# MLP phase of a two-layer kernel: layer norm and transposes of a later image spread over the turn, product 1 three blocks ahead, response norm ahead of the last splits

## The chip, the cores and the metric

The kernel runs on one core of a Trainium2 chip. The metric is the device time of one execution in microseconds, lower is better; three runs of the kernel before took 5912.92, 5915.08 and 5927.24 us (median 5915.08). The engines are TensorE (PE), VectorE (DVE), ScalarE (ACT), GpSimd (POOL) and SyncE (SP), which issues most transfers.

## The reference

The first layer is a quantized window attention on 16 images of 192 channels and 56 x 56 pixels. The second layer, the one that is concerned here, is a ConvNeXt block. Of it the phase changed here computes everything behind the depthwise convolution:

```python
mu = mean(y, -1); var = mean(square(y - mu), -1)          # over 192 channels
y = (y - mu) * rsqrt(var + 1e-6) * ln_g + ln_b
y = einsum('bhwc,cf->bhwf', y, w1) + b1                   # 192 -> 768, product 1
y = gelu(y)
gx = sqrt(sum(square(y), (1, 2)))                         # per image and feature
nx = gx / (mean(gx, -1) + 1e-6)
y = grn_g * (y * nx) + grn_b + y                          # response norm
y = einsum('bhwf,fc->bhwc', y, w2) + b2                   # 768 -> 192, product 2
out = residual + y
```

## The kernel before, in words

Eight phases follow one another; the last, `phase_mlp`, starts at 4221 us of the profiled execution. In it an image is 3136 tokens, taken as seven chunks (n = 0 to 6) of 448 tokens, and the 768 features are six blocks (f = 0 to 5) of 128. To keep fp32 precision with 16-bit operands, values are split into a high and a low fp16 part, and a product is a sum over the parts.

The phase is a software pipeline over images. Turn i computes product 2 of image i, product 1 and GELU of image i+1, and the layer norm of image i+2. A prologue does images 0 and 1 up to that point; turn 0 is written out, turns 1 to 12 are a loop, turns 13 to 15 are written out again without the parts that have no image left (`turns`, with the flags `first`, `one`, `two`, `three`).

The five engines each run their own program in order, and meet by semaphores. In a turn:

- PE (`turn` under `blk.tensor`) does for each chunk a first half, t = 0, of 18 matmuls of product 2 for output rows 0 to 127 (L1521), and a second half, t = 1, in which each block has two matmuls of product 2 for the other rows and then five of product 1 of the next image (`product1`, L1486). A product 1 block y = 6n + f waits for GELU of block y-3, because `h_psum` has three buffers. At the start of the turn PE waits for all 42 low splits of image i and for the weights. `group` (L1470) transposes two columns of 128 tokens of the layer norm's result in 6 matmuls; 14 groups make an image. Groups 0 to 2 are issued in the first half of chunk 6, 3 to 5 in its second half, 6 to 13 behind it, with `mean` (L1491), a matmul that sums over features, between them.
- ACT does GELU (L1570) and the sum of squares (L1554) of each block, copies the low sum out of `out_psum` (`low_sum`, L1561) once a chunk, and places transposed groups (`place`, L1545). `gelu` of block y waits for the low split of block y-3, because there are three `gelu` buffers. `xT_psum` has two buffers, so group x waits until group x-2 is placed.
- DVE splits each GELU block into `gelu_hi` (L1685) and `gelu_lo` (L1688) in `split`, adds product 2 to the residual (`result`, L1724, two in a chunk, and `add_low_sum`, L1730), computes the layer norm's statistics (`stats`, L1613 and L1625) and applies them (`normalize`, L1635 and L1641, in seven steps, each a seventh of the image), and computes the response norm (`response_norm`, L1695 to L1707), which folds the factor into the weights of product 2 (`w_parts`).
- POOL computes the power -0.5 of the variances (L1428), the low parts of the layer norm's result (L1433), two operations for each normalize step, and the square root in the response norm (L1438), once in a turn.
- SP loads the image for the layer norm (`z_img`), loads the residual and stores the output.

`gelu_hi` and `gelu_lo` hold one image each. Block (n, f) of image i is read by product 2 in chunk n, and the split of image i+1 writes the same place. Before the change nothing waits for that read by itself: the product 1 whose GELU is split there stands behind the read on PE.

DVE's slots are numbered 0 to 13, two in a chunk: slot 2n stands ahead of the first `result` of chunk n, slot 2n+1 ahead of its splits. Statistics have slots 2 to 8, normalize steps slots 10, 10, 11, 11, 12, 12 and 13; the response norm follows the last `result`.

```python
for f in range(NF + 1):                       # split(m, n)
    y = NF * n + f
    if f < NF:
        dve.wait_ge(hd, NH * m + y + 1)
        v.tensor_scalar(hh[:, f, cols], h[y % 3][:], kh[:], None, ALU.mult).then_inc(hhd, 1)
    if f > 0:
        dve.wait_ge(hhd, NH * m + y)
        v.scalar_tensor_tensor(hl[:, f - 1, cols], h[(y - 1) % 3][:], kh[:], hh[:, f - 1, cols], ...)
```

## Time and profile before

| | |
|---|---|
| median of 3 runs | 5915.08 us (5912.92 to 5927.24) |
| the profiled execution, its time and its span | 5934.2 us, 5932.5 us |
| mean granted PE clock | 0.824 |
| `phase_mlp` in the span | 4221 to 5932 us |
| busy in 4500 to 5000 us: PE, DVE, ACT, POOL | 440.3, 437.0, 321.9, 103.3 us |
| PE waiting for placed groups (L1545), 4430 to 5400 us | 114.3 us in 30 waits |
| DVE waiting for GELU (L1570), same stretch | 70.3 us in 184 waits |

"Busy" counts the time in which at least one instruction of the engine is under way. A granted clock of 1.00 is 2.4 GHz, 0.50 is 1.2 GHz. In the timeline a row can stand for several instructions of one kind in a row (x2, x3); a duration includes the time in which an instruction drains while the next has begun, so the pace is read from one start to the next. What stands in brackets is the idle time ahead of a row and who ended it.

### The profile page before, as it was taken

The page shows a single profiled execution, that of the slowest core. Times are in us where ns is not written, and L with a number is a line of the kernel's source. Part 1 is how long each engine was busy: PE and PEld are TensorE (multiplying, and loading weights), DVE is VectorE, ACT ScalarE, POOL GpSimd, SP SyncE. Part 2 cuts the span into 40 slices and gives each one's busy share as a digit, 9 for nine tenths or more (in the row PEclk, how much of TensorE's full clock was granted, in tenths as well). Part 3 has the DMA queues.
Part 4 walks back from the last instruction along what each step waited for, and adds up shares of the span by engine and source line. Part 5 has one row for each costly group of instructions (what it writes and reads, how often), then busy time and mean ns, then how long its engine had stood idle before and what let it go on. Part 6 is the DMA issues. An engine that isn't in the chain of part 4 may idle for free. (4 is left out here: it accounts for less than half of the span.)

```text
span 5932.5 us, 106325 instructions
## 1 busy us (share of the span) xinstructions
PE 4236.2 (71%) x34250; PEld 2544.0 (43%) x34250; DVE 4572.3 (77%) x8672; ACT 3112.4 (52%) x5458; POOL 1554.1 (26%) x1645
## 2 busy tenths in 40 slices
PE   0888994555556666666664564999578989898988
PEld 0335552222235555455553443444344444444444
DVE  6998996999999889898896453000488888888885
ACT  0756660000057677676773564444366666666664
POOL 1104330000045555555554221000121211212120
PEclk9995555555589999999997777999789989898999
DMA  7755663333332232222323777788402121221212
GB/s 295 218 144 157 194 191 78 66 65 62 61 65 75 68 77 67 74 73 68 77 58 116 260 265 249 271 287 296 139 32 94 60 94 59 77 77 66 87 64 62
DMA packets 226352, 724.94 MB, mean 122 GB/s; under 512 B 34954, under 2 KB 132746, under 8 KB 205194
## 3 DMA queue, kind: packets, MB, share of 16 engines
q1 hardware_dynamic: 182346, 524.67, 30.7%
q0 software_dynamic: 43584, 195.21, 9.7%
q8 instruction: 197, 3.23, 0.2%
q14 instruction: 225, 1.84, 0.1%
HBM read 428.25 MB, written 291.50 MB: 121 GB/s over the span
## 5 line engine op out<-in xcount | busy, mean ns | idle before, releaser
L862 ACT ACTIVATE attn_int<-p_psum,scalars 128x588 int8<-128x588 f32 x512 | 384.7, 751 | 1175.3 <-PE p_psum L534 1174.2
L786 POOL TENSOR_TENSOR exp_lo<-exp,exp_hi 128x294 f16<-128x294 f32 x1024 | 827.3, 831 | 648.4 <-ACT exp_hi L856 646.8
L1570 ACT ACTIVATE gelu<-h_psum,b_rows,w_unscale 128x448 f32<-128x448 f32 x672 | 486.2, 724 | 509.1 <-PE h_psum L1486 345.6
L1521 PE MATMUL out_psum<-gelu_hi,w_parts 128*128 128x448 f16 x2016 | 621.5, 363 | 8.2 <-DVE w_parts L1707 4.4
L827 PE MATMUL o_psum<-a_v,exp_hi 128*128 128x68 f16 x3072 | 287.1, 202 | 447.2 <-DVE a_o L907 439.4
L534 PE MATMUL range_psum<-q_diag,k_diag 128*128 128x196 bf16 x1536 | 365.4, 374 | 330.3 <-DVE p_min L652 328.1
L1613 DVE BATCH_NORM_STATS2 ln_stats<-z_img 128x6 f32<-128x192 f32 x448 | 125.5, 337 | 548.0 <-DMA z_img<-zd 548.0
L1486 PE MATMUL h_psum<-ln_parts_T,w_hi 128*128 128x448 f16 x2016 | 501.1, 358 | 20.1 <-DVE w_in L1676 16.3
L881 DVE SCALAR_TENSOR_TENSOR logit_int<-attn_int,scalars,bias_products 128x588 f16<-128x588 int8 x512 | 445.9, 871 | 88.8 <-issue 56.9
L1283 PE MATMUL conv_psum<-c_in,toeplitz 128*128 128x448 f16 (+1 forms) x2304 | 469.2, 365 | 61.9 <-DMA dwb<-in_L_conv_dw_b_dram 61.9
L1521 PE MATMUL out_psum<-gelu_lo,w_parts 128*128 128x448 f16 x1344 | 484.7, 361 | 0.0
L1688 DVE SCALAR_TENSOR_TENSOR gelu_lo<-gelu,h_scale,gelu_hi 128x448 f16<-128x448 f32 x672 | 457.3, 694 | 0.0
L827 PEld LDWEIGHTS o_psum<-a_v,exp_hi 128*128 128x128 f16 x3072 | 221.8, 101 | 517.1 <-DVE a_o L907 480.2
L1685 DVE TENSOR_SCALAR gelu_hi<-gelu,h_scale 128x448 f16<-128x448 f32 x672 | 320.0, 485 | 141.1 <-ACT gelu L1570 130.3
L534 PEld LDWEIGHTS range_psum<-q_diag,k_diag 128*128 128x128 bf16 x1536 | 181.8, 160 | 513.5 <-DVE p_min L652 510.2
L855 ACT ACTIVATE exp<-l_psum,scalars 128x588 f32<-128x588 f32 x512 | 381.6, 745 | 22.5 <-PE l_psum L813 21.6
L856 ACT ACTIVATE exp_hi<-l_psum,scalars 128x588 f16<-128x588 f32 x512 | 392.7, 767 | 0.0
L652 DVE TENSOR_TENSOR p_max<-range_psum,p_max 128x588 f32<-128x588 f32 x512 | 387.2, 756 | 0.0
L652 DVE TENSOR_TENSOR p_min<-range_psum,p_min 128x588 f32<-128x588 f32 x512 | 387.1, 756 | 0.0
L1297 ACT ACTIVATE c_out<-conv_psum,dwb,conv_unscale 128x448 f32<-128x448 f32 x192 | 223.6, 1165 | 307.1 <-PE conv_psum L1283 307.1
L1554 ACT ACTIVATE gelu_square<-gelu 128x448 f32<-128x448 f32 x672 | 380.2, 566 | 0.0
L1486 PE MATMUL h_psum<-ln_parts_T,w_lo 128*128 128x448 f16 x1344 | 370.6, 358 | 0.0
(307 smaller groups left out, 9779.2 us busy)
## 6 DMA issues: line engine op xcount, KB each, us to landing
k_diag<-kd SPq DMA_DIRECT2D x128, 384.0 KB, 5.1
toeplitz<-gd SPq DMA_DIRECT2D x48, 1024.0 KB, 16.5
yd<-y_out POOLq DMA_DIRECT2D x16, 2880.0 KB, 26.9
c_in<-yd SPq DMA_DIRECT2D x24, 1920.0 KB, 9.2
zd<-c_out POOLq DMA_DIRECT2D x24, 1792.0 KB, 13.8
z_img<-zd SPq DMA_DIRECT2D x16, 2688.0 KB, 9.8
x_chunk<-in_x_dram SPq DMA_DIRECT2D x12, 3136.0 KB, 9.8
x_img<-in_x_dram SPq DMA_DIRECT2D x16, 2352.0 KB, 16.0
```

The source lines that it names most:

```text
L534: last = nc.tensor.matmul(out[:, g, 0:HG * N], kt[:, g].rearrange("p o n -> p (o n)")[:, j::UP], q[:, g, :, j * N:(j + 1) * N], start=True ...
L652: v.tensor_tensor(e[:], ps[:, j % 4, 0:G, 0:HG * N], e[:], op).then_inc(done, 1)
L786: last = nc.gpsimd.tensor_tensor(el[r][:, :, a, 0:N], src[:, :, a], eh[r][:, :, a, 0:N], ALU.subtract)
L827: last = nc.tensor.matmul(po[:, b * PV0:(b + 1) * PV0], x[r][:, b].rearrange("p a n -> p (a n)"), rhs, start=x is eh, stop=x is el)
L856: nc.scalar.activation(eh[r][:].rearrange("p b a n -> p a b n")[:, :, :, 0:N], pl[:, bank, 0:HM].rearrange("p (a b n) -> p a b n", a=2, b= ...
L862: nc.scalar.activation(a1[l % 2][:].rearrange("p (g n) -> p g n", g=G), pp[:, 0:G, 0:HG * N], ACT.Copy, scale=col(s, CP)).then_inc(a1d, 1)
L881: v.scalar_tensor_tensor(a2[r][:], a1[(l - LAG_A2) % 2][:], col(s, RAT), s.bpart[:], ALU.mult, ALU.add).then_inc(a2d, 1)
L1283: last = nc.tensor.matmul(out[:, :, lo:hi], tp[k][:, w, ch, 2 - d, :], yi[k][:, :, ch, yy, lo + d:hi + d], start=x == 0 and part == 0, sto ...
L1486: last = nc.tensor.matmul(ph[:, y % 3, 0:TCH], w, xx, start=x == 0, stop=x == 4)
L1521: last = nc.tensor.matmul(po[:, t, 0:TCH], w, hx[:, f, cols], start=f == 0 and x == 0, stop=f == NF - 1 and x == len(steps) - 1)
L1570: nc.scalar.activation(h[y % 3][:], ph[:, y % 3, 0:TCH], ACT.Gelu, scale=k1[:], bias=b1[:, f:f + 1]).then_inc(hd, 1)
L1688: v.scalar_tensor_tensor(hl[:, f - 1, cols], h[(y - 1) % 3][:], kh[:], hh[:, f - 1, cols], ALU.mult, ALU.subtract).then_inc(hld, 1)
```

## The change

Eight things change, all in `phase_mlp`.

- The layer norm of an image is spread. In the loop, normalize steps of image i+2 stand in slots 0 to 6, and statistics, now of image i+3, in slots 9, 9, 10, 10, 11, 11, 12. Turn 0 does the statistics of image 2 in slots 0 to 3, its normalize steps in slots 5 to 8, and the statistics of image 3 in slots 10 to 13.
- PE transposes groups 2k and 2k+1 behind product 1 blocks 6k+7 and 6k+9, at most one group behind a block, and ACT places them at the same block numbers. Group 13 stands behind the last block.
- Product 1 is issued three blocks earlier relative to product 2: behind block b of product 2 stands product 1 of block b+3, and behind the last three blocks stand blocks 0 to 2 of the image after. The prologue issues three blocks more.
- Each high split waits in addition until product 2 has read the same block of the image before (`block_read`, new semaphore `gelu_block_read`).
- Product 2 waits for the low splits of its own chunk, not of the whole image.
- ACT copies the low sum of chunk n behind GELU of block 6n+8, three blocks later.
- The response norm stands behind split 3 of chunk 6; splits 4 and 5 follow the last `result`. PE's `mean` stands behind block 4 of chunk 6.
- SP issues the next `z_img` load behind the store of chunk 2 (3 in turn 0), not at the end of the turn.

```diff
-        EARLY0, EARLY, MEAN_AT = 3, 6, 10
-        TURN_STATS, TURN_NORM = 2, (10, 10, 11, 11, 12, 12, 13)
+        AHEAD, LAST = 3, 4
+        STATS_AT, NORM_AT, NEXT_STATS_AT = (0, 0, 1, 1, 2, 2, 3), (5, 5, 6, 6, 7, 7, 8), (10, 10, 11, 11, 12, 12, 13)
+        TURN_NORM_AT, TURN_STATS_AT = range(LG), (9, 9, 10, 10, 11, 11, 12)
+        group_at = [NF * (x // 2 + 1) + 1 + 2 * (x % 2) for x in range(NG)]
+        first_group_at = [max(at, 4 * NF - 2 + x) for x, at in enumerate(group_at)]
...
+                    if three and n == (3 if first else 2):
+                        sp.wait_ge(xnd, ROWP * i + 3 * ROWP)
+                        zload(i + 3)
...
-                if three:
-                    sp.wait_ge(xnd, ROWP * i + 3 * ROWP)
-                    zload(i + 3)
...
             def turn(i, first, one, two, three):
+                if first:
+                    deviation(i + 2)
                 if two:
-                    normalize(i + 2)
+                    low_parts(i + 2)
+                if three:
+                    deviation(i + 3)
                 if one:
                     root(i + 1)
...
-                if y == 0:
-                    pe.wait_ge(xtd, NG * m + NG)
+                if f == 0:
+                    pe.wait_ge(xtd, NG * m + 2 * n + 2)
...
+            for y in range(AHEAD):
+                product1(1, y, False)
+
+            def ahead(i, y, first, one, two):
+
+                if y < NH:
+                    if one:
+                        product1(i + 1, y, False)
+                elif two:
+                    product1(i + 2, y - NH, False)
+                for x in range(NG):
+                    if two and y == min((first_group_at if first else group_at)[x], NH + AHEAD - 1):
+                        group(i + 2, x, False)
 
             def turn(i, first, one, two, three):
-                pe.wait_ge(hld, NH * i + NH)
                 pe.wait_ge(w2d, 2 * i + 1)
                 for n in range(NTC):
                     cols = slice(n * TCH, (n + 1) * TCH)
+                    pe.wait_ge(hld, NH * i + NF * n + NF)
                     for t in range(2):
                         y = 2 * n + t
...
-                            if one and t == 1:
-                                product1(i + 1, NF * n + f, False)
-
-                            if two and y == MT - 2 and f >= NF - EARLY0:
-                                group(i + 2, f - (NF - EARLY0), False)
-                            if two and y == MT - 1 and f < EARLY - EARLY0:
-                                group(i + 2, EARLY0 + f, False)
-                for x in range(EARLY, NG + 1):
-                    if one and x == MEAN_AT:
-                        mean(i + 1)
-                    if two and x < NG:
-                        group(i + 2, x, False)
+                            elif t == 1:
+                                last.then_inc(ofd, 1)
+                            if t == 1:
+                                ahead(i, NF * n + f + AHEAD, first, one, two)
+                            if one and y == MT - 1 and f == NF - 2:
+                                mean(i + 1)
...
             def turn(i, first, one, two, three):
-                for y in range(NH):
-                    n, f = y // NF, y % NF
-                    if two and y == NH - NF:
-                        for x in range(EARLY0):
+                at = first_group_at if first else group_at
+                for y in range(NH + AHEAD):
+                    if one and y < NH:
+                        gelu(i + 1, y, False)
+                    if y == NH + AHEAD - 1:
+                        low_sum(i, NTC - 1, first)
+                    for x in range(NG):
+                        if two and y == min(at[x], NH + AHEAD - 1):
                             place(i + 2, x)
-                    if one:
-                        gelu(i + 1, y, False)
-                    if f == NF - 1:
+                    n = (y - NF + 1 - AHEAD) // NF
+                    if y % NF == (NF - 1 + AHEAD) % NF and 0 <= n < NTC - 1:
                         low_sum(i, n, first)
-                    if two and n == NTC - 1 and f < EARLY - EARLY0:
-                        place(i + 2, EARLY0 + f)
-                if two:
-                    for x in range(EARLY, NG):
-                        place(i + 2, x)
...
+                if not (isinstance(m, int) and m == 0):
+                    dve.wait_ge(trd, NG * m - NG + 2 * x + 2)
...
-                if x == 0 and not early:
-                    dve.wait_ge(trd, NG * m)
...
-            def split(m, n):
+            def block_read(i, n, f):
+
+                if f < NF - 1:
+                    dve.wait_ge(ofd, (NF - 1) * (NTC * i + n) + f + 1)
+                else:
+                    dve.wait_ge(om, MT * i + 2 * n + 2)
+
+            def split(m, n, before=None, lo=0, hi=NF):
 
                 cols = slice(n * TCH, (n + 1) * TCH)
-                for f in range(NF + 1):
+                for f in range(lo, hi + 1):
                     y = NF * n + f
-                    if f < NF:
+                    if f < hi:
                         dve.wait_ge(hd, NH * m + y + 1)
+                        if before is not None:
+                            block_read(before, n, f)
                         v.tensor_scalar(hh[:, f, cols], h[y % 3][:], kh[:], None, ALU.mult).then_inc(hhd, 1)
-                    if f > 0:
+                    if f > lo:
...
-            def response_norm(m):
+            def response_norm(m, before=None):
...
+                    if before is not None:
+                        block_read(before, NTC - 1, fs.stop - 1)
                     glink(v.tensor_copy(w2p[:, fs, 0:C], w2f[:, fs]))
...
-            def layernorm(m, slot):
-                if TURN_STATS <= slot < TURN_STATS + LG:
-                    stats(m, slot - TURN_STATS)
+            def layernorm(i, slot, first, two, three):
                 for x in range(LG):
-                    if TURN_NORM[x] == slot:
-                        normalize(m, x, False)
+                    if first and STATS_AT[x] == slot:
+                        stats(i + 2, x)
+                    if two and (NORM_AT if first else TURN_NORM_AT)[x] == slot:
+                        normalize(i + 2, x, False)
+                    if three and (NEXT_STATS_AT if first else TURN_STATS_AT)[x] == slot:
+                        stats(i + 3, x)
 
             def turn(i, first, one, two, three):
                 for n in range(NTC):
-                    if two:
-                        layernorm(i + 2, 2 * n)
+                    layernorm(i, 2 * n, first, two, three)
                     if n > 0:
                         add_low_sum(i, n - 1)
                     result(i, 2 * n)
-                    if two:
-                        layernorm(i + 2, 2 * n + 1)
+                    layernorm(i, 2 * n + 1, first, two, three)
                     if one:
-                        split(i + 1, n)
+                        split(i + 1, n, i, 0, NF if n < NTC - 1 else LAST)
+                    if one and n == NTC - 1:
+                        response_norm(i + 1, i)
                     result(i, 2 * n + 1)
                 if one:
-                    response_norm(i + 1)
+                    split(i + 1, NTC - 1, i, LAST)
                 add_low_sum(i, NTC - 1)
```

Three places show the new order, in the loop's turn; names in brackets are what the instruction waits for.

PE at the end of the turn, before: the last product 1 block of chunk 6 (`h_psum`), then the groups (`xT_psum`) and the mean matmul.

```order
L1486 MATMUL h_psum<-ln_parts_T,w_hi 128x448 [waits gelu_done]
L1486 MATMUL h_psum<-ln_parts_T,w_hi 128x448 x2
L1486 MATMUL h_psum<-ln_parts_T,w_lo 128x448 x2
L1465 REGISTER_ALU
L1467 REGISTER_ALU [waits ln_lo_done]
L1470 MATMUL xT_psum<-ident_f,ln_parts 128x128 [waits xT_placed]
L1470 MATMUL xT_psum<-ident_f,ln_parts 128x128 x5
L1467 REGISTER_ALU
L1470 MATMUL xT_psum<-ident_f,ln_parts 128x128 [waits xT_placed]
...
L1490 ISA
L1491 MATMUL mean_psum<-grn_sum,ones_f 128x1 [waits grn_chain]
```

The same place in the changed kernel, from the next to last group to the end of the loop.

```order
L1483 MATMUL xT_psum<-ident_f,ln_parts 128x128 [waits xT_placed]
L1483 MATMUL xT_psum<-ident_f,ln_parts 128x128 x5
L1503 ISA
L1504 MATMUL mean_psum<-grn_sum,ones_f 128x1 [waits grn_chain]
L1547 MATMUL out_psum<-gelu_hi,w_parts 128x448
L1547 MATMUL out_psum<-gelu_lo,w_parts 128x448
L1499 MATMUL h_psum<-ln_parts_T,w_hi 128x448 [waits gelu_done]
L1499 MATMUL h_psum<-ln_parts_T,w_hi 128x448 x2
L1499 MATMUL h_psum<-ln_parts_T,w_lo 128x448 x2
L1480 REGISTER_ALU
L1483 MATMUL xT_psum<-ident_f,ln_parts 128x128 [waits xT_placed]
L1483 MATMUL xT_psum<-ident_f,ln_parts 128x128 x5
```

The mean matmul stands ahead of the last two product 2 matmuls, and one group is left behind them.

ACT at the seam of chunks 0 and 1, before; the numbers are those of the three `gelu` buffers, `w1_rows<-out_psum` is the low sum.

```order
L1570 ACTIVATE gelu0<-h_psum,b1_rows,w1_unscale 128x448 [waits squares_done,gelu_lo_done,h_product]
L1554 ACTIVATE gelu_square0,sum_squares<-gelu2 128x448 [waits squares_done,gelu_done]
L1565 REGISTER_ALU
L1570 ACTIVATE gelu1<-h_psum,b1_rows,w1_unscale 128x448 [waits squares_done,gelu_lo_done,h_product]
L1554 ACTIVATE gelu_square1,sum_squares<-gelu0 128x448 [waits squares_done,gelu_done]
L1565 REGISTER_ALU
L1570 ACTIVATE gelu2<-h_psum,b1_rows,w1_unscale 128x448 [waits squares_done,gelu_lo_done,h_product]
L1554 ACTIVATE gelu_square0,sum_squares<-gelu1 128x448 [waits squares_done,gelu_done]
L1558 ISA
L1560 REGISTER_ALU [waits out_product]
L1561 COPY w1_rows<-out_psum 64x448 [waits out_whole]
```

The changed kernel: `gelu0` to `gelu2` here are blocks 6 to 8 of the next image, so the low sum of chunk 0 stands behind the third GELU of chunk 1, with a placed group ahead.

```order
L1590 ACTIVATE gelu0<-h_psum,b1_rows,w1_unscale 128x448 [waits squares_done,gelu_lo_done,h_product]
L1574 ACTIVATE gelu_square1,sum_squares<-gelu2 128x448 [waits squares_done,gelu_done]
L1590 ACTIVATE gelu1<-h_psum,b1_rows,w1_unscale 128x448 [waits squares_done,gelu_lo_done,h_product]
L1574 ACTIVATE gelu_square0,sum_squares<-gelu0 128x448 [waits squares_done,gelu_done]
L1562 ISA
L1565 COPY ln_parts_T<-xT_psum 128x3x224 [waits x_transposed]
L1590 ACTIVATE gelu2<-h_psum,b1_rows,w1_unscale 128x448 [waits squares_done,gelu_lo_done,h_product]
L1574 ACTIVATE gelu_square1,sum_squares<-gelu1 128x448 [waits squares_done,gelu_done]
L1578 ISA
L1580 REGISTER_ALU [waits out_product]
L1581 COPY w1_rows<-out_psum 64x448 [waits out_whole]
```

The low sum moved behind three more GELU blocks, and a group is placed between.

DVE at the end of the turn, before: the last splits, the last `result`, then the response norm (`grn_factor` to `w_parts`) and the low sum.

```order
L1684 REGISTER_ALU
L1685 TENSOR_SCALAR gelu_hi<-gelu,h_scale 128x448 [waits gelu_done]
L1688 SCALAR_TENSOR_TENSOR gelu_lo<-gelu,h_scale,gelu_hi 128x448 [waits gelu_hi_done] x2
L1721 REGISTER_ALU
L1724 SCALAR_TENSOR_TENSOR residual<-out_psum,out_unscale,residual 64x448 [waits out_product]
L1695 TENSOR_REDUCE grn_factor<-sum_squares 128x6 [waits squares_done]
...
L1707 TENSOR_TENSOR w_parts<-w_scaled,w_parts 128x3x128
L1727 REGISTER_ALU
L1730 SCALAR_TENSOR_TENSOR residual<-w_rows,out_unscale,residual 64x448 [waits out_done,low_sum_copied]
```

The changed kernel: the response norm begins behind low split 3, and two high and two low splits follow it.

```order
L1712 TENSOR_SCALAR gelu_hi<-gelu,h_scale 128x448 [waits gelu_block_read]
L1715 SCALAR_TENSOR_TENSOR gelu_lo<-gelu,h_scale,gelu_hi 128x448 [waits gelu_hi_done] x2
L1721 REGISTER_ALU
L1722 TENSOR_REDUCE grn_factor<-sum_squares 128x6 [waits squares_done]
...
L1736 TENSOR_TENSOR w_parts<-w_scaled,w_parts 128x3x128
L1753 SCALAR_TENSOR_TENSOR residual<-out_psum,out_unscale,residual 64x448 [waits out_product]
L1699 REGISTER_ALU [waits gelu_done]
L1712 TENSOR_SCALAR gelu_hi<-gelu,h_scale 128x448 [waits gelu_block_read]
L1712 TENSOR_SCALAR gelu_hi<-gelu,h_scale 128x448 [waits out_product,gelu_done]
L1715 SCALAR_TENSOR_TENSOR gelu_lo<-gelu,h_scale,gelu_hi 128x448 [waits gelu_hi_done] x2
L1759 SCALAR_TENSOR_TENSOR residual<-w_rows,out_unscale,residual 64x448 [waits out_done,low_sum_copied]
```

Splits 4 and 5 and the last `result` moved behind the response norm, and each high split has two waits.

## Rows read from the trace of the kernel before

**Rows 1.** POOL timeline, once-a-turn operation. Columns: start us, duration us, engine, line, operation.
```profile
4459.35 1.33 POOL L1438 TENSOR_TENSOR grn_x<-grn_factor,exponents 128x6 f32<-128x6 f32 x1 [6.08 <-DVE grn_factor L1695]
...
5790.56 1.32 POOL L1438 TENSOR_TENSOR grn_x<-grn_factor,exponents 128x6 f32<-128x6 f32 x1 [6.08 <-DVE grn_factor L1695]
5880.08 1.32 POOL L1438 TENSOR_TENSOR grn_x<-grn_factor,exponents 128x6 f32<-128x6 f32 x1 [88.19 <-DVE grn_factor L1695]
```

**Rows 2.** PE timeline, chunk 5 and the start of chunk 6 of turn 6.
```profile
5034.89 0.54 PE L1521 MATMUL out_psum<-gelu_hi,w_parts 128*128 128x448 f16 x2
...
5038.67 0.73 PE L1486 MATMUL h_psum<-ln_parts_T,w_hi 128*128 128x448 f16 x3
...
5046.24 0.54 PE L1521 MATMUL out_psum<-gelu_hi,w_parts 128*128 128x448 f16 x2
```

**Rows 3.** DVE timeline, end of the prologue, then turn 6.
```profile
4358.75 0.56 DVE L1641 CAST ln_parts<-ln_out 128x768 f16<-128x768 f32 x1
...
5006.44 1.12 DVE L1613 BATCH_NORM_STATS2 ln_stats<-z_img 128x6 f32<-128x192 f32 x4
...
5007.76 0.78 DVE L1685 TENSOR_SCALAR gelu_hi<-gelu,h_scale 128x448 f16<-128x448 f32 x2
...
5035.85 0.45 DVE L1685 TENSOR_SCALAR gelu_hi<-gelu,h_scale 128x448 f16<-128x448 f32 x1 [0.28 <-ACT gelu L1570]
5036.22 1.27 DVE L1688 SCALAR_TENSOR_TENSOR gelu_lo<-gelu,h_scale,gelu_hi 128x448 f16<-128x448 f32 x2
5037.41 0.67 DVE L1724 SCALAR_TENSOR_TENSOR residual<-out_psum,out_unscale,residual 64x448 f32<-64x448 f32 x1
...
5049.27 1.71 DVE L1685 TENSOR_SCALAR gelu_hi<-gelu,h_scale 128x448 f16<-128x448 f32 x2
5050.90 1.08 DVE L1688 SCALAR_TENSOR_TENSOR gelu_lo<-gelu,h_scale,gelu_hi 128x448 f16<-128x448 f32 x1
...
5057.33 1.24 DVE L1635 TENSOR_SCALAR ln_out<-z_img,ln_mean_var,ln_rstd 128x192 f32<-128x192 f32 x4
...
5059.07 2.43 DVE L1635 TENSOR_SCALAR ln_out<-z_img,ln_mean_var,ln_rstd 128x192 f32<-128x192 f32 x4
...
5073.62 0.18 DVE L1695 TENSOR_REDUCE grn_factor<-sum_squares 128x6 f32<-128x42 f32 x1
...
5079.19 0.75 DVE L1704 TENSOR_TENSOR w_scaled<-w_in,grn_factor 128x576 f32<-128x576 f32 x1
```

**Rows 4.** PE timeline, the end of turn 6 and the next turn's start.
```profile
5048.51 0.50 PE L1470 MATMUL xT_psum<-ident_f,ln_parts 128*128 128x128 f16 x6
...
5057.05 0.82 PE L1470 MATMUL xT_psum<-ident_f,ln_parts 128*128 128x128 f16 x6 [6.57 <-ACT ln_parts_T L1545]
...
5079.40 0.92 PE L1521 MATMUL out_psum<-gelu_hi,w_parts 128*128 128x448 f16 x2 [0.37 <-DVE w_parts L1707]
```

**Rows 5.** Windows view: window us, length, PE busy (instructions), granted clock, DMA share, GB/s.
```profile
5057.00:5061.00 4.00, 3.95 (x20) 0.50 0.00 0
```

**Rows 6.** POOL timeline, one normalize step's two low parts.
```profile
5049.43 2.07 POOL L1433 TENSOR_TENSOR ln_parts<-ln_out,ln_parts 128x512 f16<-128x512 f32 x2 [1.08 <-DVE ln_parts L1641]
```

**Rows 7.** ACT timeline, turn 6, chunks 5 and 6.
```profile
5035.71 0.56 ACT L1554 ACTIVATE gelu_square<-gelu 128x448 f32<-128x448 f32 x1
...
5036.40 0.53 ACT L1561 COPY w_rows<-out_psum 64x448 f32<-64x448 f32 x1
...
5052.07 0.72 ACT L1570 ACTIVATE gelu<-h_psum,b_rows,w_unscale 128x448 f32<-128x448 f32 x1 [8.32 <-issue]
...
5053.25 0.71 ACT L1570 ACTIVATE gelu<-h_psum,b_rows,w_unscale 128x448 f32<-128x448 f32 x1
...
5062.61 0.72 ACT L1570 ACTIVATE gelu<-h_psum,b_rows,w_unscale 128x448 f32<-128x448 f32 x1 [0.20 <-PE h_psum L1486]
...
5064.39 0.73 ACT L1570 ACTIVATE gelu<-h_psum,b_rows,w_unscale 128x448 f32<-128x448 f32 x1
```

**Rows 8.** Page, DMA issues: transfer, queue, count, KB each, us from issue to landing.
```profile
z_img<-zd SPq DMA_DIRECT2D x16, 2688.0 KB, 9.8
```

12 lines of the change are left out of this document (8 added, 4 removed).

## The prediction

> **What bounds the kernel now.** I read the views in this order: the POOL timeline for the length of a turn, the PE timeline for its inner rhythm, then what ended PE's idle time, and last the DVE and ACT timelines beside it. The seven earlier phases end at 4221 us and are not touched, so only the last phase counts. Its turns are told apart by the POOL operation that occurs once in each [rows 1]: thirteen periods take 1331.2 us, 102.4 us each, and the one after them, without layer norm, 89.5 us.
>
> Inside a turn PE works through seven chunks. A chunk is 11.35 us from start to start [rows 2]: 3.4 us of product 2 for output rows 0 to 127 (first half), then six blocks of 1.325 us, in each two matmuls of product 2 (0.38 us) and five of product 1 (0.95 us) (second half). DVE, by contrast, may be far behind: the splits of chunk 5 begin at 5049.27 [rows 3], three microseconds after PE has left that chunk, and PE lost nothing in the chunk by it. PE runs at its rate in five chunks of seven; the time above the rate is at the end of the turn, where it waits 6.57 us for a transpose group [rows 4], again while ACT places groups, and then for the response norm. The clock then stands at 0.50, the 1.2 GHz level, for 4 us of product work [rows 5]. Seven chunks at the rate are 79.5 us and fourteen transpose groups 4.6 us (0.33 each: 0.50 busy, less the 0.17 by which a matmul's record outlasts its issue) [rows 4]: 84.1 of 102.4 us.
>
> **What the change removes.** The lump at the end goes: no PE wait on placed groups, and the squares and the response norm no longer wait for splits 40 and 41. Before, the stretch from the start of chunk 6 to the next turn is 5046.24 to 5079.40, 33.2 us [rows 2, 4]; chunk 0 behind it, partly at 1.2 GHz, takes 12.5 us (102.4 less 33.2 less five chunks).
>
> **What it adds.** PE issues product 1 of block b+3 behind block b. The rings stay at three `h_psum` and three `gelu` buffers, so that product waits for gelu b, and gelu b waits for low split b-3. At block 3 of a chunk (b counted within it) PE therefore waits for the low split of block 0 of the same chunk. Before, product b waited for gelu b-3 and so for low split b-6: a whole chunk of slack, which the lateness of 5049.27 used. PE is in order, so blocks 4 and 5 of product 2 stand behind the waiting product, and DVE's high splits 4 and 5 now wait for these two to be read. Each engine waits for the other once in a chunk. ACT, too, places a group after gelu 1 of a chunk and copies the low sum only after gelu 2, and the second half's product 2 waits for that copy.
>
> **The walk through a steady turn.** Time 0 is the end of PE's issue of the chunk before. Durations, start to start: high split 0.37, low split 0.59, result 0.59 [rows 3]; one stats step 1.32 [rows 3]; one normalize step 1.74 alone (5057.33 to 5059.07), 2.95 straight behind another (2.43 + 0.5) and, with two residual operations between, the middle of these, 2.35 [rows 3], since POOL's low parts of the step before run some 2 us beside it [rows 6]; gelu to gelu on ACT 1.78 with a placed group between, 1.17 without [rows 7].
> - DVE is free at 1.44: product 2 of block 5 is complete at -0.75, then high, low, low, result (2.15).
> - The low sum is copied at 4.13: low split 4 ends 0.34, gelu 1 at 0.43, square and group to 2.22, gelu 2, square, copy of 0.53. PE's second half starts there, not at 3.41: 0.7 us in chunks 1 to 6.
> - From the first high split (S) to PE's product at block 3: two highs and a low, gelu 0.72 and the hops between: 2.28 us, or 3.59 with POOL busy (5049.27 to the gelu of 5052.07 is 2.80, plus 0.79) [rows 3, 7]. Behind it PE needs 3.94 us, and 0.45 more where a placed group delays gelu 4.
>
> Chunk 0: DVE comes 5.3 late from the response norm (second weight half 2.3 [rows 3], result, four splits, low sum); normalize 7.0, result 7.6, normalize S = 10.0; 10.0 + 3.59 + 3.94 = 17.5.
> Chunks 1 and 2: normalize 3.2; low sum from 4.13 to 5.1 (a residual operation with two SBUF inputs beside POOL, taken like the low split, 1.08 for 0.68 [rows 3]); result 5.7; normalize S = 7.45; + 3.59 + 4.39 = 15.4 each.
> Chunk 3: one normalize, S = 5.7, no wait: 4.13 + 7.95 + two groups 0.66 = 12.7.
> Chunk 4: result 5.3, two stats steps (the first without aggregates) S = 7.65; + 2.28 + 4.39 = 14.3.
> Chunk 5: four stats steps, S = 7.95; 14.6.
> Chunk 6: second half from 4.13, product 2 of block 3 read at 9.0, low split 2 done 10.1, gelu 41 and both squares from there, 1.17 + 0.66 [rows 7], to 12.0; from the sum of squares to PE's next turn 5.78 us (5073.62 to 5079.40 [rows 3, 4]): 17.8.
> Sum: 17.5 + 30.8 + 12.7 + 14.3 + 14.6 + 17.8 = 107.8 us (107.9 unrounded).
>
> **The clock.** In chunk 0 PE stands still for 3.6 to 5 us before block 3. After 6.57 us of idling it ran at 1.2 GHz for 4 us, costing 1.9 [rows 4, 5]. Bounds 0 and 1.9 per turn; that wait is shorter than the row's, so I take the middle, 1.0. A steady turn is then 108.9, 6.5 above before; twelve of them +78.
>
> **The other turns.** Turn 0 does the layer norm of two images. Its statistics now stand ahead of everything, and their `z_img` load is issued when DVE's last normalize before it ends, near 4358.7 [rows 3]; at 9.8 us to landing [rows 8] DVE is held to about 4368.8. The same walk gives chunks of 16.1, 13.1, 16.1, 21.8, 15.0, 14.8 and 18.4, and 1 for the clock: end at about 4480.6, against 4465.0 before (5079.40 less six periods): +16. Turn 13 has no statistics: 105.4 against 102.3, +3. Turn 14 has no layer norm and no groups, its chunks run at 11.35 and only chunk 6 pays (16.8): 85.5 against 89.5, -4. Turn 15 is the same. The prologue's three early products (2.9 us) lie in the wait for `z_img`.
>
> Nothing for the load of image i+3: it is issued 4.8 us into chunk 3, lands 9.8 later, and its first statistics are 18 us into that chunk. The second wait of each high split I take at zero when it is met: ACT's gelu has three waits and keeps a pitch of 1.17 [rows 7]; the upper end is the hop of 0.09 from low split to gelu for each of 42, 3.8 us a turn, and is in the range.
>
> Total +78 + 16 + 3 - 4 = +93. The profiled execution took 5934.2 us (span 5932.5 and 1.7 around it) and would take 6027; it lay 19.1 above the median, and I put the change on the median: 5915.1 + 93 = 6008 us.
>
> **A rule to weigh.** A low split beside POOL took 1.08 us in place of 0.68 [rows 3], and I charged the low sum of chunks 1 and 2 the same 0.4. The Trainium skill ("SBUF — State Buffer", section "SBUF: two separate sides") says that the pair of ports that VectorE and GpSimd share is locked for a whole instruction, by VectorE also for two SBUF inputs. By that rule the low sum could be held until POOL is through, up to 0.3 us longer in each of the two chunks, and the sum would be about 7 us higher; the trace's 1.08 shows a partial hold and not which of the two it would be here.
>
> **Rivals.**
> 1. *Each engine is limited by its own work.* If the ring of three gives enough slack, a turn costs DVE's own work (splits 40.3, results and low sums 12.4, stats 9.6, normalizes with their delays 19.5, response norm 7.9, total 89.7) and some 4 us at the seam: 94. For it: before, DVE's lateness cost PE nothing in the middle chunks. Against it: that slack was six blocks and is now three. 12 x -8.4, turn 0 +6, turns 13 and 14 -14: -109, 5806 us. Faster; chance 0.14.
> 2. *The waits partly close.* If the spread steps meet POOL's low parts less than the rows suggest (2.28 for 3.59 and no 0.4), chunks 0, 1 and 2 lose 1.3, 1.7, 1.7; if the low sum also comes 0.7 earlier in chunks 1 to 6, the turn is about 101 to 103. With turn 0 that is 5905 to 5940, centre 5922. For it: the POOL rows overlap only where steps are close. Against: the walk puts them as close as before. Chance 0.16.
> 3. *The clock falls in every waiting chunk.* Chunks 1, 2, 4 and 5 wait 1 to 3.4 us each; if each then ran 4 us at 1.2 GHz, 6 to 8 us a turn come on top: 6008 + 84 = 6092. It decides from the point where 2 to 3 us of waiting is enough; the rows show the fall only after 6.57. Chance 0.08.
> 4. *My walk, with terms off by some tenths per chunk:* 108.9 +- 3 a turn, 5965 to 6050. Chance 0.62.
>
> **Numbers.** Predicted 6008; the range 5905 to 6060 takes in the last and most of the second, leaving out the first, and much of the third. A measurement of this kernel cannot tell less than 0.3% (18 us) from none. Slower: 0.62 + 0.08 + 0.07 of the second = 0.77; same 0.06; faster 0.14 + 0.03 = 0.17.
>
> **What the profile after would show.** Right: the POOL period near 109; PE's largest waits at the product-1 line, ended by ACT's gelu, once a chunk in chunks 0, 1, 2, 4, 5; DVE's high split waiting for product 2; the PE wait for placed groups gone. Wrong: a period below 102, PE waiting chiefly for the weight parts and DVE busy without gaps; or a second half that starts at 3.4 us, which would refute the low-sum term; or high splits beside POOL of 0.45 us, which would refute the port term.

## The result and the profile after

The changed kernel took 6057.5 us, median of 3 runs (6049.7 to 6058.9), against 5915.1: ratio 1.0231, 95% interval 1.0206 to 1.0257. It is slower, as forecast. The forecast was 6008 us in a range of 5905 to 6060; the measured 142 us are half as much again as the 93 predicted, and the time lies only 2.5 us inside the upper end of the range. The 5915.1 is a median of three runs; in the later comparisons the same kernel had medians of 5929 to 5933 us (7 to 21 runs each), so up to some 16 of the 142 us may lie in those three runs.

The profiled execution took 6058.85 us, 124.7 more than that of before. First the length of a turn, from the POOL timeline, to be laid beside [rows 1] (columns: start us, duration us, engine, line, operation):

```profile
4323.90 1.38 POOL L1445 TENSOR_TENSOR grn_x<-grn_factor,exponents 128x6 f32<-128x6 f32 x1 [63.95 <-DVE grn_factor L1722]
4469.46 1.32 POOL L1445 TENSOR_TENSOR grn_x<-grn_factor,exponents 128x6 f32<-128x6 f32 x1 [1.49 <-DVE grn_factor L1722]
...
5810.86 1.32 POOL L1445 TENSOR_TENSOR grn_x<-grn_factor,exponents 128x6 f32<-128x6 f32 x1 [4.36 <-DVE grn_factor L1722]
5917.77 1.32 POOL L1445 TENSOR_TENSOR grn_x<-grn_factor,exponents 128x6 f32<-128x6 f32 x1 [45.82 <-DVE grn_factor L1722]
6004.58 1.32 POOL L1445 TENSOR_TENSOR grn_x<-grn_factor,exponents 128x6 f32<-128x6 f32 x1 [85.49 <-DVE grn_factor L1722]
```

Turn 0 is 145.6 us long (before 127.2), the twelve steady turns 1341.4 or 111.8 each (before 102.4), then 106.9 (102.3) and 86.8 (89.5). The differences, +18.4, +112.5, +4.6 and -2.7, make +133 us in this phase. The first of these POOL operations came 8 us earlier in this execution than before: the layer norm of the phase's start came 9 us earlier, behind stages that are the same in both, and what follows it took 1 us more.

What ended the waits, from 4800 to 5600 us, seven turns (columns: engine, operation, what it waited for; us in total, times, longest; rows of PE and DVE, others left out at the dots):

```profile
PE h_psum L1499 <- ACT gelu L1590: 90.3, 63, 6.9
DVE gelu_hi L1712 <- PE out_psum L1547: 65.6, 99, 2.2
DVE residual L1759 <- ACT w_rows L1581: 42.0, 35, 2.9
...
PE out_psum L1547 <- ACT w_rows L1581: 22.9, 42, 0.8
...
PE mean_psum L1504 <- DVE grn_sum L1724: 21.3, 8, 2.7
...
DVE ln_out L1655 <- issue: 12.9, 8, 1.7
```

The wait for placed groups [rows 4] is gone. In its place PE waits at product 1 for ACT's gelu, and DVE's high split waits for PE: each for the other, as foretold. The PE timeline shows where (turn 6; the idle time before a row stands in brackets):

```profile
5028.58 0.59 PE L1504 MATMUL mean_psum<-grn_sum,ones_f 128*128 128x1 f32 x2 [2.67 <-DVE grn_sum L1724]
...
5032.56 0.55 PE L1547 MATMUL out_psum<-gelu_hi,w_parts 128*128 128x448 f16 x2 [0.37 <-DVE w_parts L1736]
...
5047.95 1.30 PE L1499 MATMUL h_psum<-ln_parts_T,w_hi 128*128 128x448 f16 x3 [6.93 <-ACT gelu L1590]
...
5054.00 0.54 PE L1547 MATMUL out_psum<-gelu_hi,w_parts 128*128 128x448 f16 x2
...
5058.07 0.36 PE L1547 MATMUL out_psum<-gelu_hi,w_parts 128*128 128x448 f16 x1 [0.50 <-ACT w_rows L1581]
...
5064.78 0.74 PE L1499 MATMUL h_psum<-ln_parts_T,w_hi 128*128 128x448 f16 x3 [1.85 <-ACT gelu L1590]
...
5069.19 0.54 PE L1547 MATMUL out_psum<-gelu_hi,w_parts 128*128 128x448 f16 x2
...
5084.38 0.54 PE L1547 MATMUL out_psum<-gelu_hi,w_parts 128*128 128x448 f16 x2
...
5097.08 0.54 PE L1547 MATMUL out_psum<-gelu_hi,w_parts 128*128 128x448 f16 x2
...
5111.74 0.54 PE L1547 MATMUL out_psum<-gelu_hi,w_parts 128*128 128x448 f16 x2
...
5126.25 0.54 PE L1547 MATMUL out_psum<-gelu_hi,w_parts 128*128 128x448 f16 x2
...
5144.23 0.62 PE L1547 MATMUL out_psum<-gelu_hi,w_parts 128*128 128x448 f16 x2 [0.40 <-DVE w_parts L1736]
```

Chunk 0 starts at 5032.56; the rows at 5054.00, 5069.19, 5084.38, 5097.08, 5111.74 and 5126.25 are the first product 2 matmuls of chunks 1 to 6, and the last row is the start of the next turn. The second half of chunk 1 starts at 5058.07, 4.07 behind its first.

| chunk | 0 | 1 | 2 | 3 | 4 | 5 | 6 |
|---|---|---|---|---|---|---|---|
| predicted, us | 17.5 (+1.0 clock) | 15.4 | 15.4 | 12.7 | 14.3 | 14.6 | 17.8 |
| measured, us | 21.4 | 15.2 | 15.2 | 12.7 | 14.7 | 14.5 | 18.0 |

Six chunks of seven lie within 0.4 us of the walk. Chunk 0 is 2.9 longer than its 18.5. The DVE timeline, to be laid beside [rows 3], shows one part of that:

```profile
5037.16 0.67 DVE L1759 SCALAR_TENSOR_TENSOR residual<-w_rows,out_unscale,residual 64x448 f32<-64x448 f32 x1
5039.46 1.25 DVE L1655 TENSOR_SCALAR ln_out<-z_img,ln_mean_var,ln_rstd 128x192 f32<-128x192 f32 x4 [1.62 <-issue]
...
5041.81 2.06 DVE L1655 TENSOR_SCALAR ln_out<-z_img,ln_mean_var,ln_rstd 128x192 f32<-128x192 f32 x4
...
5044.38 1.71 DVE L1712 TENSOR_SCALAR gelu_hi<-gelu,h_scale 128x448 f16<-128x448 f32 x2
5046.00 1.08 DVE L1715 SCALAR_TENSOR_TENSOR gelu_lo<-gelu,h_scale,gelu_hi 128x448 f16<-128x448 f32 x1
...
5050.79 0.45 DVE L1712 TENSOR_SCALAR gelu_hi<-gelu,h_scale 128x448 f16<-128x448 f32 x1 [1.71 <-PE out_psum L1547]
...
5058.05 0.89 DVE L1759 SCALAR_TENSOR_TENSOR residual<-w_rows,out_unscale,residual 64x448 f32<-64x448 f32 x1 [0.82 <-ACT w_rows L1581]
```

Before its first normalize DVE idles 1.62 us for nothing but "issue". The first high split therefore starts 11.8 us into the turn, and not at 10.0. Turn 1, the loop's first, is the control: it has no such gap (PE row of its start, then DVE rows):

```profile
4474.89 0.93 PE L1547 MATMUL out_psum<-gelu_hi,w_parts 128*128 128x448 f16 x2 [0.73 <-DVE w_parts L1736]
```

```profile
4480.00 1.24 DVE L1655 TENSOR_SCALAR ln_out<-z_img,ln_mean_var,ln_rstd 128x192 f32<-128x192 f32 x4
...
4484.91 1.71 DVE L1712 TENSOR_SCALAR gelu_hi<-gelu,h_scale 128x448 f16<-128x448 f32 x2
```

Its first high split starts 10.0 us in, as predicted. In turn 6, behind PE's stall the high split waits 1.71 for PE in turn. The windows view shows the other part (granted clock: third number from the right):

```profile
5029.00:5030.00 1.00, 1.00 (x4) 0.43 (x5) 0.62 (x4) 0.00 (x0) 0.00 (x0) 0.50 0.00 0
...
5032.00:5033.00 1.00, 0.63 (x7) 0.28 (x5) 1.00 (x2) 0.72 (x1) 0.00 (x0) 1.00 0.00 0
...
5048.00:5049.00 1.00, 1.00 (x3) 0.38 (x4) 1.00 (x3) 1.00 (x4) 0.00 (x0) 0.50 0.00 0
...
5052.00:5053.00 1.00, 1.00 (x10) 0.68 (x9) 0.00 (x0) 1.00 (x2) 0.00 (x0) 0.87 0.00 0
```

Behind the wait of 6.93 us PE works at 1.2 GHz until about 5052: product 1 and two blocks take 6.05 us (5047.95 to 5054.00) where 3.94 were reckoned. Together 1.8 + 2.1 - 1.0 (the clock term of the sum) = 2.9 us. Over the twelve steady turns chunk 0 takes 19.2 us in turn 1 and 20.7 to 22.3 in the others, 21.5 in the mean, 3.0 above 18.5.

### The profile page after: what moved, and what is told of

It is laid out like the page before. It is cut to its first block and busy times, and to the rows that moved or that the text cites. A ratio compares the mean times of both kernels' runs of the same rounds, so it can differ in the third digit from the quotient of the medians.

```text
span 6056.8 us, 107252 instructions
## 1 busy us (share of the span) xinstructions
PE 4259.9 (70%) x34250; PEld 2508.2 (41%) x34250; DVE 4540.7 (75%) x8672; ACT 3073.2 (51%) x5458; POOL 1556.1 (26%) x1645
## 3 DMA queue, kind: packets, MB, share of 16 engines
q14 instruction: 226, 1.85, 0.1%
## 5 line engine op out<-in xcount | busy, mean ns | idle before, releaser
L1499 PE MATMUL h_psum<-ln_parts_T,w_hi 128*128 128x448 f16 x2016 | 514.2, 365 | 205.3 <-ACT gelu L1590 186.8
L1440 POOL TENSOR_TENSOR ln_parts<-ln_out,ln_parts 128x512 f16<-128x512 f32 x224 | 231.2, 1052 | 661.5 <-DVE ln_parts L1659 661.5
L855 ACT ACTIVATE exp<-l_psum,scalars 128x588 f32<-128x588 f32 x512 | 381.7, 745 | 23.6 <-PE l_psum L813 22.3
```

The lines of the kernel that those rows point to most:

```text
L1499: last = nc.tensor.matmul(ph[:, y % 3, 0:TCH], w, xx, start=x == 0, stop=x == 4)
```

## The experiments

Ratios are to the kernel before, run on the same chip; "a turn" is the mean of the twelve steady ones in the profiled execution, from the once-a-turn POOL operation as above. The lead is the number of blocks by which product 1 is issued ahead of product 2; the response norm is early when it stands ahead of splits 4 and 5 of chunk 6, and last when it stands behind them.

| kernel | lead | gelu buffers | response norm | a turn, us | ratio (95%) |
|---|---|---|---|---|---|
| before | 0 | 3 | last | 102.4 | 1 |
| changed | 3 | 3 | early | 111.8 | 1.0231 (1.0206 to 1.0257) |
| ahead2 | 2 | 3 | early | 102.8 | 1.0012 (0.9999 to 1.0025) |
| ahead1 | 1 | 3 | early | 100.7 | 0.9958 (0.9937 to 0.9978) |
| ahead0 | 0 | 3 | early | 102.6 | 1.0014 (0.9997 to 1.0031) |
| spread_only | 0 | 3 | last | 102.1 | 1.0005 (0.9987 to 1.0023) |
| gelu_ring6 | 3 | 6 | early | 94.2 | 0.9837 (0.9815 to 0.9859) |
| lead1_gelu6 | 1 | 6 | early | 97.5 | 0.9901 (0.9870 to 0.9933) |
| gelu6_norm_last | 3 | 6 | last | 95.9 | 0.9879 (0.9855 to 0.9904) |
| gelu6_low_early | 3 | 6 | early | 94.5 | 0.9823 (0.9798 to 0.9848) |
| before_gelu6 | 0 | 6 | last | 102.3 | 0.9996 (0.9979 to 1.0013) |
| low_early | 3 | 3 | early | 109.2 | 1.0161 (1.0137 to 1.0186) |
| pool_light | 3 | 3 | early | 107.0 | 1.0129 (1.0110 to 1.0148) |
| norm_later | 3 | 3 | early | 110.9 | 1.0199 (1.0169 to 1.0229) |

**The lead.** Three kernels change one number (with lead 0 the mean's product also moves behind the last block, since it needs every gelu).

```diff
-        AHEAD, LAST = 3, 4
+        AHEAD, LAST = 2, 4        # ahead2; 1 in ahead1, 0 in ahead0
```

> Lead of two blocks (AHEAD 2). Ring theory: the wait moves from block 3 to block 4 of a chunk, 1.325 us less behind it in five chunks, and up to 1 us for the clock: 104 to 106 us a turn, total 5950 to 5975 us. Spread theory: no change of more than 10 us from 6057.

> Lead of one block (AHEAD 1). Ring theory: product 1 behind block b waits for low split b-5, so only block 5 of a chunk can wait for a split of the same chunk; what is left behind the wait is 2.65 us shorter than with a lead of three in each of chunks 0, 1, 2, 4, 5: 13 us a turn off, and 1 to 2 for the clock: 97 to 100 us, total 5860 to 5900 us. Spread theory: no change of more than 10 us from 6057.

> Product 1 again directly behind its own block (AHEAD 0), the mean behind the last of them; spread layer norm and early response norm kept. Ring theory (the three-block lead in rings of three costs the time): the wait inside each chunk goes, a turn is DVE's own work plus the seam, 93 to 97 us for 112.2, total 5810 to 5870 us. Rival, spread theory (the spread normalize steps beside POOL's low parts and the shifted response norm cost the time, not the lead): a turn stays at 107 us or more, total 6000 or more.

The spread theory falls with all three: with the normalize steps and the response norm where the change put them, a turn is 9 to 11 us shorter as soon as the lead is. The first step, from three to two, gave 9.0 us (102.8 a turn, 104 to 106 expected); the next gave only 2.1 more (100.7, with 97 to 100 expected), and the last took 1.9 back. All three totals missed what was expected: 5940, 5908 and 5941 us for 5950 to 5975, 5860 to 5900 and 5810 to 5870. A lead of one with three buffers is 0.4% faster than the kernel before. Here the ring theory, as I had it, failed: it expected 93 to 97 us for lead 0. The rows of ahead0 show what was overlooked (PE, then DVE timeline):

```profile
4919.23 0.36 PE L1547 MATMUL out_psum<-gelu_hi,w_parts 128*128 128x448 f16 x1 [1.87 <-DVE residual L1753]
```

```profile
4879.31 0.20 DVE L1722 TENSOR_REDUCE grn_factor<-sum_squares 128x6 f32<-128x42 f32 x1 [2.36 <-ACT gelu_square L1574]
...
4915.69 0.45 DVE L1712 TENSOR_SCALAR gelu_hi<-gelu,h_scale 128x448 f16<-128x448 f32 x1 [0.75 <-ACT gelu L1590]
```

PE stands nowhere at product 1, and it waits for DVE's residual operation instead (61.8 us in 32 waits from 4800 to 5600 us): DVE is the bound. But DVE itself waits, up to 0.75 for a gelu (47.1 us in 77 waits, some 6 us a turn) and 2.36 for the last square. With three buffers gelu b needs low split b-3 whatever the lead is. I read the waits so, that ACT can't get ahead of DVE when a group has to be placed, and that the work of the two engines adds up at these places; a run with no lead and six buffers, which would test it, is missing.

spread_only takes the early response norm away too, so that of the change the spread layer norm, the spread groups and the waits that go with them are left. Expected were 101 to 102 us a turn and a ratio of 0.995 to 1.001; measured were 102.1 and 1.0005. Spreading by itself neither costs nor gains here.

**The ring.** Six gelu buffers, with nothing else of the order changed. With nothing moved they do not fit: 192 bytes a partition are lacking (4608 needed for the last buffer, 4416 left). The room comes from one buffer of squares, laid into `w1_rows`, and half a `w2_scaled`; the number must divide the 42 blocks of an image.

```diff
-        h = [sb(f"gelu{k}", [P, TCH], F32) for k in range(3)]
+        h = [sb(f"gelu{k}", [P, TCH], F32) for k in range(6)]
...
-                if not (early and y < 3):
-                    act.wait_ge(hld, NH * m + y - 2)
+                if not (early and y < 6):
+                    act.wait_ge(hld, NH * m + y - 5)
```

> Lead of three kept, six gelu buffers for three (the room comes from one buffer of squares, placed in the unused w1_rows, and a w_scaled half as long; the h_psum ring stays at three). Ring theory: gelu b then waits for low split b-6, as many blocks back as with no lead and three buffers, so PE no longer stands inside the chunks and high splits 4 and 5 no longer wait for product 2. What is left of a turn is DVE's row of work: 88.5 us busy in every trace so far, 1.6 of loop turn-around, 1.5 + 0.35 + up to 2.4 in the response norm: 93 to 97 us for 112.2, total 5830 to 5880 us. Rival, PSUM theory (the three h_psum banks, with product 1 queued in front of product 2, are the limit whatever stands behind them): the PE wait at product 1 stays and the total is within 30 us of 6057.

Measured: 94.2 us a turn, ratio 0.9837, where the lead of three with three buffers had 1.0231. The PSUM theory falls: the three `h_psum` banks are the same, and PE's wait at product 1 is gone from the list. DVE is now back to back (timeline, chunk 0 of a turn):

```profile
4944.82 1.71 DVE L1712 TENSOR_SCALAR gelu_hi<-gelu,h_scale 128x448 f16<-128x448 f32 x2
4946.45 1.09 DVE L1715 SCALAR_TENSOR_TENSOR gelu_lo<-gelu,h_scale,gelu_hi 128x448 f16<-128x448 f32 x1
4947.46 0.44 DVE L1712 TENSOR_SCALAR gelu_hi<-gelu,h_scale 128x448 f16<-128x448 f32 x1
4947.82 0.67 DVE L1715 SCALAR_TENSOR_TENSOR gelu_lo<-gelu,h_scale,gelu_hi 128x448 f16<-128x448 f32 x1
4948.42 0.44 DVE L1712 TENSOR_SCALAR gelu_hi<-gelu,h_scale 128x448 f16<-128x448 f32 x1
```

A block costs it 0.96 us from high split to high split, without a bracket; and the windows view gives 87.4 us of DVE work in a stretch of 94.2 (fourth number; PE's, the second, is 87.2):

```profile
4928.00:5022.20 94.20, 87.19 (x499) 46.27 (x500) 87.43 (x212) 64.25 (x147) 20.53 (x16) 0.96 0.24 78
```

Ten idle gaps of DVE, from 0.24 to 1.78 us, make up the other 6.8 us; the two longest are the one before the first normalize and the 1.50 for POOL in the response norm.

Is it the buffers alone? And what do lead and norm add once the ring is six long?

> The kernel before with six gelu buffers (room made in the same way), nothing else changed. Ring theory of the pair (the lead makes the ring matter; the lump of layer norm, groups and response norm at the end is what holds the kernel before): product 1 behind block b waits there for low split b-6 already, so PE's waits for the groups and the weight parts stay: 100 to 102.4 us a turn, ratio to before 0.98 to 1.00. Rival (the gain of six buffers belongs to the buffers alone and the change adds nothing to it): a turn of 96 us or less, ratio 0.987 or lower with the end lump hidden.

> Lead of one block with six gelu buffers (low split b-8 is waited for). With three buffers this lead had 100.7 us a turn, of which DVE waited some 5 for gelus and 2.4 for the last square. Ring theory: with three more buffers ACT runs ahead of DVE and both go: 93 to 96 us a turn, total 5810 to 5860 us. If DVE's gelu waits come from the order of PE and ACT and not from the ring (rival), the turn stays at 100 to 101 and the total at 5900 to 5915.

> Lead of three and six gelu buffers, but the response norm again behind the last splits, and the mean's product behind the last block (LAST 6). In the lead-three ring-of-six kernel DVE is the bound, 94.1 us a turn, and PE waits 1.0 for the mean, 1.7 and 0.5 for the weight parts and 3.7 for a residual operation of DVE a chunk later. If DVE stays the bound, the later weights only shorten that later wait: 94 to 96 us a turn, ratio to before 0.983 to 0.988. Rival (the early response norm is what lets the lead pay): DVE itself waits for PE's first half of the next turn, 98 us a turn or more, ratio 0.992 or more.

The kernel before gains nothing from six buffers (0.9996). PE's waits for placed groups do fall there, from 91.4 to 23.4 us in 4800 to 5600 us, but once a turn PE waits for DVE in their place (PE timeline, chunk 6):

```profile
5059.28 0.55 PE L1521 MATMUL out_psum<-gelu_hi,w_parts 128*128 128x448 f16 x1 [6.34 <-DVE residual L1726]
```

DVE, with the normalize steps in a lump, has no gap from 5040 to 5075 us, and the weight parts come no sooner. So this lump holds the turn, whatever the number of buffers. The whole change loses 2.3% without the buffers; together they give 1.6%. With the ring of six a lead of three beats a lead of one by 0.6% (my expectation of 93 to 96 for lead one missed; PE there waits up to 4.0 for the mean, and DVE 2.6 for the last square, which a lead of three hides). The early response norm is worth 0.4%, between my two bounds: DVE stays the bound, but its gap before the first normalize grows from 1.9 to 2.8 at most, and its small waits for PE become more. How much of the 1.0% of lead one belongs to the lead and how much to the spread was not tried, as no run has six buffers and no lead.

**The parts of the walk.** The low sum, moved one gelu ahead; POOL's low parts cut to a quarter; the normalize steps half a chunk later.

```diff
# low_early
-                    n = (y - NF + 1 - AHEAD) // NF
-                    if y % NF == (NF - 1 + AHEAD) % NF and 0 <= n < NTC - 1:
+                    n = (y - NF + 2 - AHEAD) // NF          # and ahead of the placed groups
+                    if y % NF == (NF - 2 + AHEAD) % NF and 0 <= n < NTC - 1:
# pool_light: this leaves out part of the computation
-                    src, rows = xn[x % 2], slice(4 * x, 4 * x + 4)
+                    src, rows = xn[x % 2][:, 0:n], slice(4 * x, 4 * x + n)      # n = 1 from image 2
# norm_later
-        TURN_NORM_AT = range(LG)
+        TURN_NORM_AT = range(1, LG + 1)
```

> As the changed kernel (lead 3, three buffers), but ACT copies a chunk's low sum one gelu earlier, ahead of the placed group. By the walk of the prediction the second half of product 2 starts 0.5 to 0.7 us earlier in chunks 1 to 6, and the low sum's residual operation with it, which sets the first high split: 3 to 4 us a turn, total 6000 to 6025 us. If the low sum is not on the path (DVE held by its own work or by PE's stall alone), less than 10 us.

> As the changed kernel, but from image 2 on POOL computes the low parts of only one row in four of each layer norm step (the others keep older values: this leaves out part of the computation). Port theory (VectorE operations beside POOL's low parts are stretched, and the ring passes the whole delay on): the second normalize of a pair falls from 2.07 to about 1.25, two high splits from 1.71 to 0.80, a low split from 1.08 to 0.68, so chunks 0, 1, 2 each lose about 2.1 to 2.4 us and chunk 3 about 1: 7 to 8 us a turn, total 5950 to 5970 us. If POOL's company costs little, under 20 us.

> As the changed kernel (lead 3, three buffers), each normalize step half a chunk later: chunk 0 has one of them and chunk 3 two. Walk: DVE's first high split of chunk 0 comes 2.5 us earlier, PE's 6.9 us wait there shrinks to about 4.4; chunk 3 turns from 13.0 to about 15.2. If the wait of 6.9 us is what drops the clock in chunk 0, and 4.4 does not, another 2 us go: 110 us a turn, total 6030, ratio to before 1.018 to 1.020. If the clock stays as it is: 112 us, total 6050 to 6060, ratio 1.022 to 1.025.

low_early: 2.6 us a turn less, 0.7% by the ratios (some 41 us); slightly under 3 to 4, and its 6031 us miss the 6000 to 6025, but far over the rival's 10 us in total: the late low sum is on the path. Its PE rows have no wait for `w_rows` left, and part of the gain comes back at block 3 (2.02 there in place of 1.85). The rest of what is missing is the clock: chunk 1 of a turn takes 14.7 us and chunk 2, with the same wait, 15.9 (both 15.2 in the changed kernel), as it runs at 1.2 GHz behind it (PE and windows rows, chunk 2):

```profile
5074.62 0.98 PE L1499 MATMUL h_psum<-ln_parts_T,w_hi 128*128 128x448 f16 x3 [2.02 <-ACT gelu L1590]
```

```profile
5076.00:5078.00 2.00, 2.00 (x6) 0.76 (x5) 0.87 (x2) 2.00 (x6) 0.00 (x0) 0.50 0.00 0
```

This happens in one waiting chunk of each of the twelve turns (chunk 1 in two of them, chunk 2 in ten) and costs 1.2 to 1.4 us. Without it the gain would have been 3.8 us a turn, within the expectation.

pool_light: 4.8 a turn less, for 7 to 8 expected. Its chunk 1 (PE timeline, to be laid beside the wait of 1.85 above):

```profile
5040.33 0.36 PE L1547 MATMUL out_psum<-gelu_hi,w_parts 128*128 128x448 f16 x1 [0.50 <-ACT w_rows L1581]
5045.73 0.74 PE L1499 MATMUL h_psum<-ln_parts_T,w_hi 128*128 128x448 f16 x3 [0.55 <-ACT gelu L1590]
...
5054.21 0.36 PE L1547 MATMUL out_psum<-gelu_hi,w_parts 128*128 128x448 f16 x1 [0.50 <-ACT w_rows L1581]
```

The chunk is 13.9 us long for 15.2. High split pair (0.98 for 1.71), low split (0.72 for 1.08) and low sum (0.68 for 0.89) give 1.3 us, which is that difference. My expectation had charged the second normalize of chunks 1 and 2 too; its rows are 1.23 there with and without POOL's load, since operations lie between it and the first. Only in chunk 0 does it meet POOL (2.06). Chunk 3 does not change (12.7), as PE is its bound.

norm_later: 110.9 us a turn, between the two expectations, and its interval overlaps that of the changed kernel, so the total tells nothing. The turns do, for behind the first of the twelve (108.2) they fall into two kinds, 109.4 to 109.6 and 110.8 to 112.4. PE and windows rows of one of 110.8 and one of 109.6:

```profile
5191.66 1.30 PE L1499 MATMUL h_psum<-ln_parts_T,w_hi 128*128 128x448 f16 x3 [4.24 <-ACT gelu L1590]
...
5401.52 0.93 PE L1547 MATMUL out_psum<-gelu_hi,w_parts 128*128 128x448 f16 x2 [1.40 <-DVE w_parts L1736]
...
5414.45 0.74 PE L1499 MATMUL h_psum<-ln_parts_T,w_hi 128*128 128x448 f16 x3 [2.73 <-ACT gelu L1590]
```

```profile
5192.00:5194.00 2.00, 2.00 (x7) 0.88 (x6) 1.05 (x2) 2.00 (x7) 0.00 (x0) 0.50 0.27 58
...
5402.00:5404.00 2.00, 2.00 (x7) 0.78 (x6) 1.88 (x4) 0.73 (x1) 0.00 (x0) 0.50 0.01 4
...
5414.00:5416.00 2.00, 1.55 (x9) 0.82 (x10) 1.61 (x4) 2.00 (x6) 0.00 (x0) 1.00 0.41 82
```

In the second, PE begins the turn at 1.2 GHz, so it reaches block 3 later, waits 2.73 and finds the full clock behind the wait. In the first it began at 2.4 GHz, waited 4.24 and worked at 1.2 GHz behind that. Here a slow clock ahead of the wait was absorbed by the wait, and one behind it was paid in full.

**The best version.**

> Lead of three, six gelu buffers, and the low sum copied one gelu earlier. DVE is the bound at 94.1 us a turn; its waits for the low sum and behind it for product 2 (0.71 and 0.73 in chunk 3) and for the reading of product 2 (0.2 to 0.6 each, some ten a turn) are what this can take: 92.5 to 93.5 us a turn, ratio to before 0.980 to 0.983. If they only move to another place of the chunk: 94.1, ratio 0.984.

Measured 0.9823, a turn 94.5. The two intervals (0.9798 to 0.9848 and 0.9815 to 0.9859) can't be told apart, and the turns are no shorter: with DVE as the bound its small waits move to another place. Both versions beat both kernels; what the six buffers give behind the changed order does it, and the earlier low sum adds nothing that can be told.

## Why the prediction was right in sign and short in size

- *The ring of three couples the engines.* Shown: undoing the lead or lengthening the ring takes the loss away, undoing neither leaves it.
- *The walk of chunks 1 to 6.* Right within 0.4 us each (its printed terms add up to 107.7 and not 107.8; the unrounded ones to 107.85). In chunk 1: first high split 7.2 us in (7.45 predicted), 3.58 from there to PE's product (3.59), 4.40 behind it (4.39).
- *The low sum term.* Second half at 4.07 (4.35 in chunk 4), predicted 4.13.
- *Turns 0, 13 and 14*: +18.4, +4.6, -2.7 for +16, +3, -4.
- *Mis-sized: chunk 0 and its clock.* The terms were "10.0 + 3.59 + 3.94 = 17.5" and "I take the middle, 1.0". Measured: 11.8 + 3.57 + 6.05 = 21.4. 1.6 of the 1.8 us ahead of the first split is the idle "issue" time ahead of DVE's first normalize. In turns 1 and 13, where that gap is missing, the first split came at 10.0 and 10.3. In the kernel before, the gap could not be seen, since DVE waited 2 us for PE at this place anyway:

```profile
5084.15 0.68 DVE L1724 SCALAR_TENSOR_TENSOR residual<-out_psum,out_unscale,residual 128x448 f32<-128x448 f32 x1 [1.97 <-PE out_psum L1521]
```

It moved onto the path when the change put work there. The clock term was too small even at its upper bound of 1.9: behind the wait PE needed 5.3 to 6.9 us for the 3.94, 2.3 more in the mean of the twelve turns. The length of the wait does not order them: 1.7 more behind 3.75 (turn 1), 1.3 and 1.4 behind 5.2 and 5.3 (the two turns of 110.9 us), 2.8 to 2.9 behind 5.4 to 5.5, 2.1 to 2.6 behind 6.9 to 7.2. So the middle between two bounds was a guess at a quantity that the one row of 6.57 did not bound. The steady turns together took 34.5 us more than the walk, and chunk 0 alone 36 (3.0 x 12); the others cancel to within 2.
- *The rest* of the 142: the profiled execution before lay 19 us above its median and that after 1 above, so the difference of the profiles is 125 and that of the medians 142. I had added the change to the median.
- *The edge of the range.* The walk was given 108.9 +- 3 a turn; the measured 111.8 lies at its edge, and the time 2.5 us inside 6060. The width was not worked out from the two terms that failed, so that the range held is luck in part.
- *The port rule.* The low sum of chunk 1 ran from 5058.05 for 0.89 us, 0.22 more than alone (0.67), beside this POOL row:

```profile
5057.31 2.16 POOL L1440 TENSOR_TENSOR ln_parts<-ln_out,ln_parts 128x512 f16<-128x512 f32 x2 [10.70 <-DVE ln_parts L1659]
```

It ended at 5058.94, half a microsecond ahead of POOL's row. By the rule of the Trainium skill ("SBUF — State Buffer", section "SBUF: two separate sides") it would be held until the POOL instruction then under way is through; the row holds two and does not say where the first ends, so a hold for part of the time is what is shown, smaller than the 0.4 that I charged. The 7 us that the rule would have added did not come.
- *Rival 1* (94 us a turn) described another kernel: with six buffers a turn is 94.2. The total is met better than its parts: 87.4 us of DVE work and 6.8 idle, where it had 89.7 and 4. Its condition, slack enough in the ring, is what the change lacked.
- *Rival 2* fell with the low sum and the port terms, which came as walked but for the low sum's 0.22 in place of 0.4. *Rival 3* did not come in this kernel: its waits of 1.04 to 1.88 in chunks 1, 2, 4 and 5 left the clock at 1.00. But it was near. In low_early, with waits of 2.02, the clock fell in one of these chunks in every turn. What did happen here is a second fall a turn, at the seam (below).

## What to carry to other kernels

When a producer is issued further ahead, count in blocks what it waits for: with a lead of k, three banks and N gelu buffers, the product issued behind block b needs the split of block b + k - 3 - N, and an in-order engine holds back everything queued behind that wait. Lengthen the ring together with the lead: here the change with its lead of three cost 2.3% with three buffers and gained 1.6% with six, and six buffers without the change gave 0.0%. If the ring can't grow, keep the lead short (0.4% gained with a lead of one). An idle gap that another wait covers is not free: look for it where you put work or take the cover away.
